# A graph network layer on one Trainium2 core: the descriptor scratch of dynamic DMAs at 8192 in place of 16384 bytes per partition

## What is computed

```
h = relu(layernorm(x))
e = silu(concat(h[src], h[dst], dist) @ eW1 + eb1)
e = silu(e @ eW2 + eb2)
agg = segment_sum(e, src)
x + silu(concat(h, agg) @ nW1 + nb1) @ nW2 + nb2
```

## Time and profile before

| what | value |
|---|---|
| time, median of 3 runs | 3559.34 us (3557.65 to 3560.01) |
| span of the profiled execution | 3042.3 us |
| outside the span (difference of the two) | 517.0 us |
| TensorE busy, share of the span | 87% |
| VectorE | 70% |
| GpSimd | 66% |
| ScalarE | 53% |
| mean granted TensorE clock | 0.986 |

### The profile page before, as it was taken

The page is one execution under the profiler, slowest core; times in us unless marked ns, Lnnn a source line. Parts: engine busy times, 40 slices in busy tenths (PEclk is TensorE's granted clock), DMA queues, the critical chain, the costliest instruction groups (busy, mean ns, idle before and its releaser), DMA issues.

```text
span 3042.3 us, 77490 instructions
## 1 busy us (share of the span) xinstructions
PE 2652.8 (87%) x21703; PEld 2068.1 (68%) x21704; DVE 2125.5 (70%) x7337; ACT 1601.7 (53%) x3366; POOL 2012.3 (66%) x2075
## 2 busy tenths in 40 slices
PE   7899999999688888888888888888888888888899
PEld 4555555555477777777777777777777777777776
DVE  8999999997566666666666666666666666666665
ACT  3677777777344444444444444444444444444455
POOL 1254444445677777777777777777777777777772
PEclk7999999999799999999999999999999999999999
DMA  3011111111222222222222222222222222222343
GB/s 94 20 40 27 39 28 39 34 34 30 48 59 59 60 57 59 59 60 59 58 59 59 60 60 58 58 60 59 59 59 59 59 59 58 58 59 55 77 120 103
DMA packets 366054, 171.78 MB, mean 56 GB/s; under 512 B 289494, under 2 KB 330126, under 8 KB 365934
## 3 DMA queue, kind: packets, MB, share of 16 engines
q0 software_dynamic: 69600, 123.49, 15.4%
q1 hardware_dynamic: 274142, 36.29, 7.8%
q10 hardware_dynamic: 22192, 10.53, 1.2%
HBM read 139.11 MB, written 31.04 MB: 56 GB/s over the span
## 4 chain that ended last, share of the span: by engine, by line
PE 81%; issue 11%; ACT 4%; DVE 3%; DMA 1%; POOL 0%; ACTq 0%; SPq 0%; DVEq 0%; POOLq 0%
PE bk L1208 16%; PE bk L1228 15%; PE bk L1219 13%; PE bk L1206 9%; PE bk L1196 5%; PE bk L1071 4%; PE bk L1217 3%; PE bk L1105 3%; PE bk L1137 2%; PE bk L1059 2%; PE bk L1060 2%; PE bk L1239 1%; ACT BIG L1354 1%; PE bk L1099 1%; PE bk L1274 1%
## 5 line engine op out<-in xcount | busy, mean ns | idle before, releaser
L554 POOL DMA_INDIRECT GA<-q_d,IX x1758 | 1671.5, 951 | 545.4 <-issue 533.3
L920 DVE SCALAR_TENSOR_TENSOR GA<-c_bc,EW,GA 128x128 f32<-128x128 f32 x1758 | 558.5, 349 | 432.7 <-DMA GA<-q_d,IX 429.2
L929 DVE TENSOR_TENSOR BIG<-bk,BIG 128x128 f32 x1758 | 511.4, 291 | 345.1 <-issue 156.4
L1206 PE MATMUL bk<-identf,GA 128*128 128x128 f32 x1758 | 501.2, 285 | 253.8 <-issue 240.3
L1208 PE MATMUL bk<-OHS,P 128*128 128x128 bf16 x5274 | 695.8, 225 | 0.1
L1443 ACT ACTIVATE ED<-bk,eb1c 128x512 f32<-128x512 f32 x440 | 302.1, 687 | 703.0 <-PE bk L1208 698.7
L1208 PEld LDWEIGHTS bk<-OHS,P 128*128 x5274 | 501.3, 96 | 111.3 <-issue 0.2
L1228 PE MATMUL bk<-ED 128*128 128x128 f32 x3516 | 504.7, 287 | 0.0
L519 POOL DMA_INDIRECT rec_d<-BIG,GA x208 | 246.8, 1187 | 376.9 <-issue 285.6
L1219 PEld LDWEIGHTS bk<-W,ED 128*128 128x128 f32 x3516 | 464.8, 193 | 24.3 <-issue 7.6
L1206 PEld LDWEIGHTS bk<-identf,GA 128*128 128x128 f32 x1758 | 247.5, 141 | 321.7 <-issue 297.2
(11 more groups left out here) (247 smaller groups left out, 2761.9 us busy)
## 6 DMA issues: line engine op xcount, KB each, us to landing
GA<-q_d,IX POOLq DMA_INDIRECT x1758, 2.5
q_d<-QS SPq DMA_DIRECT2D x14, 448.0 KB, 3.1
u_d<-QS ACTq DMA_DIRECT2D x98, 64.0 KB
OHS<-u_d SPq DMA_DIRECT2D x18, 256.0 KB, 3.1
rec_d<-ED SPq DMA_DIRECT2D x16, 220.0 KB, 9.6
RW<-rec_d SPq DMA_DIRECT2D x110, 32.0 KB
rec_d<-BIG,GA POOLq DMA_INDIRECT x208, 2.4
HT<-hT_d ACTq DMA_DIRECT2D x99, 32.0 KB
```

The costliest lines, as they stand in the source:

```text
L554: e.indirect_dma_start(G[k % 4 * U + u], None, q_d, bass.IndirectOffsetOnAxis(ap=IX[g // BG % 2][:, k * U + u:k * U + u + 1], axis=0))\
L920: ins = e.scalar_tensor_tensor(out=G[k % 4 * U + u], in0=c_bc[:, :], scalar=ew[:, w:w + 1], in1=G[k % 4 * U + u], op0=ALU.mult, op1=ALU.add)
L929: e.tensor_tensor(AGG[:, ds(v, P)], banks[6 + k % 2][:, u * P:(u + 1) * P], AGG[:, ds(v, P)], ALU.add).then_inc(s["ad"], 1)
L1206: e.matmul(z, G[k * U + u], identf[:, :], is_transpose=True, start=True, stop=False)
```

## The change

```diff
@@ -1520,7 +1520,7 @@
     from concourse import mybir as _mybir
     from concourse.bass_utils import run_bass_kernel_spmd as _run
 
-    nc = _bacc.Bacc("TRN2", target_bir_lowering=False, num_devices=1)
+    nc = _bacc.Bacc("TRN2", target_bir_lowering=False, num_devices=1, dynamic_dma_scratch_size=8192)
     arrays, args = {}, []
     for name in _INS:
         a = _np.ascontiguousarray(inputs[name])
```

## The result

The changed kernel takes 3564.36 us (median of 10 runs, 3561.25 to 3566.79) beside 3557.81 us (3555.39 to 3560.01) of the kernel before on the same chip: a ratio of 1.0019 [1.0011, 1.0027]. It is slower by about 6.5 us. The time lies in the range that was given, but the forecast of no difference is wrong, since the interval leaves out 1.

A forecast was written before the change was run, and what follows sets the result against it. The prediction took GpSimd's preparing of descriptors to pace the edge stage. It summed a span of 3042.3 us, 0 for the change and 517.0 us around the span to 3559.3 us, with a range of 3550 to 3572 us.

The forecast's parts named there:

- The bound: Edge stage: GpSimd, never held up, issues gathers as fast as it can for 2209.4 us, 73% of the span.
- 517.0 us to lie around the span: Outside the recorded span of 3042.3 us: 517.0 us that no record shows, taken as unchanged.
- Room in the scratch: GpSimd's descriptor scratch: half still holds the four transfers under way at worst, so no wait; price 0.
- The cost of taking space back: Releasing old scratch entries on GpSimd: taken as 0, at best 8.8 us faster over the edge stage's gathers.
- The rounds: GpSimd's gathers: twice as many rounds through the half scratch, seen as longer gathers; taken as 0, at most 12.3 us.
- The addresses: All tensors move down by 8192 bytes together: taken as 0, bounded by 12.3 us slower and 10.5 us faster.
- Rival 1: Gathers or something outside the span: faster with the smaller scratch, by 8.8 or 8.7 us; chance 0.05.
- Rival 2: GpSimd's gathers: each round costs a little, up to 12.3 us, 3571.6 us; 0.07 with Rival 3 and unlucky address.
- Rival 3: GpSimd, scratch full, waits once a round for landings, 1.25 us each, 39 us by the 56-gather estimate; chance 0.02.
- Rival 4: Descriptor rings: they keep their size or another limit holds, so time stays 3559 us; chance 0.05.

The follow-up runs named there:

- e11: Kernel before, with GpSimd writing 128x480 floats (about 0.5 us) before the third gather of each group: 3568.59 us, ratio 1.0040.
- e13: Kernel before with 8192 bytes of scratch and, from the fifth group on, only two of four gathers issued: 2611.88 us, ratio 0.8589.
- e1: The kernel before, unchanged (16384 bytes of scratch), run as if it were a change: ratio 0.9999.
- e3: The change itself (8192 bytes of scratch) run once more, against the kernel before: ratio 1.0032.
- e2: Kernel before with 8192 bytes of scratch and an unused tensor keeping tensors at old addresses (four small constants excepted): ratio 1.0031.
- e9: Kernel before with an unused tensor of 1024 bytes behind all others: ratio 0.9996.
- e10: Kernel before with an unused tensor of 1024 bytes in front of all others: ratio 1.0000.
- e15: Kernel before with 8192 bytes of scratch, GpSimd waiting before each gather until the last but one has landed: 3563.72 us, ratio 1.1722.
- e16: Kernel before with 16384 bytes of scratch, GpSimd waiting before each gather until the last but one has landed: 3556.98 us, ratio 1.1701.
- e5: Kernel before with 15360 bytes of scratch, addresses kept by an unused tensor of 1024 bytes: 3564.39 us, ratio 1.0016.
- e17: Kernel before, 16384 bytes of scratch, with one additional indirect DMA of 128 rows into an unused tensor before the first gather: ratio 1.0004.
- e14: Kernel before with 16384 bytes of scratch and, from the fifth group on, only two of four gathers issued: 2611.14 us, ratio 0.8587.
- e6: Kernel before with 17408 bytes of scratch, all tensors 1024 bytes higher: 3564.57 us, ratio 1.0014.

## Why the prediction was wrong

**The bound.** "The edge stage is paced by GpSimd's preparing of descriptors" is right for the profile that was shown. It does not hold for the runs that were timed. There GpSimd waits 1.3 to 1.4 us once a group for TensorE's announcement, which is acted on almost 3 us after the recorded matmuls, and delays inside a group are mostly absorbed (e11: 13.5 of some 170 us). The table had the warning: a time of 3559.34 beside a span of 3042.3. I took 517.0 us to lie around the span, which is a term of the sum; it measured 1.8 us. The sum 3042.3 + 0 + 517.0 came out right only because it was closed on the median.

**Room in the scratch.** Right in its figures. The estimate of 9 entries of 16 bytes to a gather and of 56 gathers in 8192 bytes, from the Trainium skill's page "DMA: Bandwidth & Descriptors", sections "Terms" and "The descriptor swizzle", is borne out here in its product of 144 bytes: the first event is at gather 56, and at 28, 106, 113 and 120 with the four other sizes. No trace shows a wait for want of room: the pauses come once a round and are longer the larger the scratch is.

**The cost of taking space back.** Here the reasoning failed. I compared transfers early and late and found equal durations and idle pieces, and concluded that the cost does not grow with what lies in the scratch. It is paid once a round, and it grows with the round: +0.39, +0.72, +1.31 and +1.46 us for rounds of 13, 41, 91 and 105 gathers. A fixed part of about 0.24 us and 0.012 us for each gather of the round fits these four, and it fits the 0.83 us of e13's rounds of 49, which had no part in it. A few rows between two events could not show it.

**The rounds.** This is the step that failed: "I take 0" for the term of the rounds, which measured 6.4 us. The mark of a round was sought in the gather's duration, and the bound of 12.3 us was worked out from it. Durations hold none of it (959 ns in e1 and e3). It lies in the idle piece ahead, and only where that piece is already a wait. In the earlier trace rows there is none to be seen, since at that pace GpSimd never pauses before a first gather. So the forecast was not to be had from that trace by looking for the mark; but "once a round" was priced as if it could fall anywhere, and where it falls decides: of 42 rounds 11 cost something. The size, 6.4 us here, lies within the bound by chance.

**The addresses.** Right: 0 (e2 as e3, e9 and e10).

**The rivals.** Rival 1 is out. Rival 2, slower by the rounds, was right in direction and nearly in size, and was given too little; its sign, longer gathers, was wrong. Rival 3's sign, idle pieces of 1.5 us and more in a regular series, is what came, with rounds of 41, but not its price: it would be 1.25 us in each of 42 rounds, and what was seen is about 0.6 us in 11. Rival 4 is out, since the distances follow the size.

**What stays open.** That a round shows where GpSimd has a wait in its program just before is seen in e15 and e16; why it is hidden elsewhere is argued, not shown. If the work of a round can run ahead while preceding gathers are being prepared, but not ahead of a wait, then about 1.2 us of it are covered before a second gather, more before a later one, and nothing before a first. The small excess before second gathers fits (+0.09, +0.17 and +0.25 us for rounds of 91, 98 and 105, none for 41 and 13). Two single pauses do not: 0.94 us before the third gather 106 in e5, and 1.89 us before the second gather 113 in e17. Why the rounds are 15 gathers shorter than the scratch is not shown either; in e13 and e14, where 8 of the 16 buffers and their semaphores are in turn, the distances are 49 (seen as multiples of 98 in e13, whose longer pauses on first gathers are at 170, 268, 366, ...) and 106, which is 7 less than 56 and 113. e15 and e16 differ by 6.7 us in their medians, but their profiled executions by 2.2 us only (3559.02 and 3556.80), with 3.5 us in the edge stage (2740.5 and 2737.0 us); how much of it the rounds make is not broken down. Why one set ran at 3040 us and four at 3510 to 3559, that is, why the announcement is acted on 2.9 us late in the one case and 0.04 us in the other, is unknown. The plain change was not timed at the pace of 3040 us; the trace of before has no event that shows, so I would expect nothing there.

## What to carry to other kernels

Before a sum is made against a profile, compare the profiled execution's own time with the timed median: a gap of 15% means two different paces, not hidden time, and the limit of a stage may differ between them. A cost that is paid once a round is not found in means or medians; number the instructions of a line, list the idle pieces that are longer than usual, and look at the distances between their numbers. Whether it costs anything depends on where it falls against the loop's own period, so a size that is free can have dearer neighbours on both sides.

## What was not expected of the hardware

- 15360 and 17408 bytes of scratch are both slower than 16384 (1.0016 and 1.0014), and 4096 no worse than 8192 (1.0030 beside 1.0031 and 1.0032).
- GpSimd pays about 0.24 us and 0.012 us for each gather of a round, seen when a round falls on a gather with a wait before it (e3 to e6, e13, e15, e16).
- The count of the rounds began anew at the first gather of the edge stage, though other indirect DMAs had gone before, and it did not begin anew after 6.39 us of idle time before gather 20.
- At the slower pace TensorE's announcement was acted on 2.87 us after the last recorded matmul in the median (e1), at the faster one 0.04 us after it.
- One and the same kernel took 3040 us in one set and 3511, 3559, 3555 and 3511 in the others, with a granted clock of 0.985 and about 0.91 over the span. With at most two gathers under way it took 3557 us in the set of 3040 as well, but not by this delay: it is 0.04 us in e16 too.
